# Spectral block of a four-image convolution: two of the four output rows of a Winograd tile computed on GpSimd instead of VectorE

## What is computed

```python
f = fft2(x)                                   # over the two image axes
amp, phase = abs(f), angle(f)
mod_amp = amp * sigmoid(amp @ w_h + b_h) + amp * sigmoid(amp @ w_l + b_l)
spatial = real(ifft2(mod_amp * exp(1j * phase)))
conv = conv3x3(spatial, w_f) + b_f            # SAME padding, 128 -> 128 channels
y = swish(conv) + x
y = (y - mean(y)) * rsqrt(var(y) + 1e-3) * gamma + beta   # over the channels
```

## Time and profile before

| | |
|---|---|
| median of 3 runs | 4309.92 us (4308.83 to 4311.2) |
| the profiled execution: its own time | 4313.71 us |
| its span in the trace | 4311.8 us |
| TensorE busy over the span | 3997.2 us (93%) |
| VectorE busy | 3525.8 us (82%) |
| ScalarE busy | 3160.2 us (73%) |
| GpSimd busy | 2583.8 us (60%) |
| convolution stage of the first image | about 236 to 450 us from the start |
| the fourth image's, the last | about 1509 to 1725 us |

### The profile page before, as it was taken

One profiled execution on the slowest core, in us unless ns is written; L12 is line 12 of the kernel. 1 busy time (PEld: TensorE's weight loads), 2 busy tenths in 40 slices (PEclk: granted clock), 3 DMA queues, 4 the chain that ended last, 5 costly groups with the idle time before them and its releaser, 6 DMA issues.

```text
span 4311.8 us, 95150 instructions
## 1 busy us (share of the span) xinstructions
PE 3997.2 (93%) x31687; PEld 2864.0 (66%) x31687; DVE 3525.8 (82%) x8840; ACT 3160.2 (73%) x4900; POOL 2583.8 (60%) x2713
## 2 busy tenths in 40 slices
PE   7898889789979996599999999999999999999998
PEld 4687568757875786366666666666666666666665
DVE  4568456745775577599999999999999999999997
ACT  4345524552455255599999999999999999999997
POOL 0036103610360047488888888888888888888886
PEclk9999999999999998799999999999999999999999
DMA  2013101400140022111111111111111111111110
GB/s 90 1 51 124 62 1 54 151 32 2 62 165 10 2 65 88 41 40 41 39 41 39 41 39 41 39 41 39 41 39 41 39 41 39 41 39 41 39 41 25
DMA packets 214867, 205.94 MB, mean 48 GB/s; under 512 B 14369, under 2 KB 149153, under 8 KB 214689
## 3 DMA queue, kind: packets, MB, share of 16 engines
q1 hardware_dynamic: 214688, 203.60, 14.4%
HBM read 136.45 MB, written 67.11 MB: 47 GB/s over the span
## 4 chain that ended last, share of the span: by engine, by line
PE 58%; DVE 0%; ACT 0%; POOL 0%; issue 0%; POOLq 0%; DVEq 0%; ACTq 0%
PE g_ps L1039 7%; PE g_ps L1024 6%; PE g_ps L982 6%; PE g_ps L968 5%; PE g_ps L1027 5%; PE g_ps L1056 5%; PE g_ps L999 3%; PE g_ps L1069 3%; PE g_ps L1075 3%; PE g_ps L1048 3%; PE g_ps L1008 3%; PE g_ps L973 3%; PE g_ps L988 2%; PE g_ps L1064 2%; PE g_ps L961 2%; PE g_ps L993 1%
## 5 line engine op out<-in xcount | busy, mean ns | idle before, releaser
L1351 DVE TENSOR_TENSOR g_mmat<-g_emat,g_ps 128x1024 f32<-128x1024 f32 x512 | 599.6, 1212 | 3.7 <-PE g_ps L999 2.7
L1190 ACT ACTIVATE g_emat<-g_ps 128x1024 f32<-128x1024 f32 x512 | 521.3, 1025 | 90.1 <-PE g_ps L1027 88.6
L1294 DVE SCALAR_TENSOR_TENSOR g_acc<-g_ps,g_conv_w,g_acc 128x504 f32<-128x504 f32 (+1 forms) x768 | 555.2, 723 | 11.4 <-ACT g_acc L1153 9.5
L869 POOL TENSOR_TENSOR g_acc<-g_acc,g_tap 128x508 f32<-128x508 f32 x384 | 482.0, 1270 | 128.1 <-DVE g_acc L1294 128.1
L609 POOL MEMSET f_s_hi<- 128x192 f32 x4 | 1.0, 258 | 851.9 <-PE f_ps L344 851.9
L1039 PEld LDWEIGHTS g_ps<-g_mmat,g_dtx 128*32 128x32 f32 x8192 | 192.8, 109 | 310.5 <-issue 164.3
L1024 PE MATMUL g_ps<-g_rz,g_l 128*128 128x512 f32 x1024 | 389.4, 461 | 1.6 <-DVE g_z L1379 1.6
L229 PE MATMUL f_ps<-f_s_hi,f_wf_hi 128*128 128x256 f32 x1152 | 360.7, 313 | 5.0 <-DVE f_s_lo L456 5.0
L1039 PE MATMUL g_ps<-g_mmat,g_dtx 128*32 128x128 f32 x8192 | 329.3, 279 | 0.0
L230 PE MATMUL f_ps<-f_s_lo,f_wf_hi 128*128 128x256 f32 x1152 | 326.5, 283 | 0.0
L231 PE MATMUL f_ps<-f_s_hi,f_wf_lo 128*128 128x256 f32 x1152 | 326.1, 283 | 0.0
(11 more groups left out here) (194 smaller groups left out, 12380.7 us busy)
## 6 DMA issues: line engine op xcount, KB each, us to landing
f_xt<-in_x_cols SPq DMA_DIRECT2D x32, 1024.0 KB, 10.6
f_xres<-in_x SPq DMA_DIRECT2D x128, 256.0 KB, 2.7
z<-f_zout SPq DMA_DIRECT2D x128, 256.0 KB, 2.0
g_zin<-z SPq DMA_DIRECT2D x128, 256.0 KB, 2.6
g_zres<-z SPq DMA_DIRECT2D x128, 256.0 KB, 2.8
out<-g_outb SPq DMA_DIRECT2D x128, 256.0 KB, 2.9
f_wf_raw<-in_w_f SPq DMA_DIRECT2D x1, 576.0 KB, 6.8
g_wx<-in_in_proj_t SPq DMA_DIRECT2D x1, 192.0 KB, 2.4
```

The lines of the kernel that those rows point to most:

```text
L869: pool.tensor_tensor(acc[:, j, :, 1:], acc[:, j, :, 1:], tap1[:, j, :, 0:P - 1], ALU.add).then_inc(add_p[j], 1)
L1190: act.activation(emat[:, g, :].rearrange("p (b n) -> p b n", b=2), ps[:, D_BANK[g]:D_BANK[g] + 2, :], ACT.Exp).then_inc(e_a[g], 1)
L1294: dve.scalar_tensor_tensor(out=acc[:, j, :, k:], in0=four(ps[:, bank, :])[:, :, 0:P - k], scalar=conv_w[:, j, 3 - k:4 - k], in1=acc[:, j, ...
L1351: dve.tensor_tensor(mmat[:, g, :].rearrange("p (h n) -> p h n", h=HEADS), emat[:, g, :].rearrange("p (h n) -> p h n", h=HEADS), ps[:, CB, ...
```

## The change

In `tile_rows` the two instructions L470 and L473 (rows 2 and 1) go. GpSimd gets a new function `inner_rows(k)` of four instructions, which makes the same two rows: two `tensor_scalar` (0.25 * sums near, 0.5 * diffs near, 256 elements each, into `scaled`, a slot of `work` that this stage did not use), a wait for both, and two `tensor_tensor` additions into `conv_y` with the same interleaved writes. It stands last in GpSimd's round k, behind `affine(k-3, ...)` and `root(k-2)`; GpSimd's loop now starts at k = 0. It waits for `sum_done` and `diff_done` of VectorE and for the transposes of batch k-2. Two waits are new elsewhere: `silu(k)` on ScalarE also waits for `inner_done` of batch k, and `tile_rows(k)` on VectorE, before it writes `sums` again, for `inner_done` of batch k-1.

```diff
+        scaled = work[:, 3, :].rearrange("p (a n) -> p a n", a=2)
...
                 def silu(k):
                     act.wait_ge(y_done[k % 2], b * 8 + (k // 2 + 2))
+                    act.wait_ge(inner_done, b * BATCHES + (k + 1))
...
                 dve.wait_ge(mids_ready, done)
+                if k:
+                    dve.wait_ge(inner_done, b * BATCHES + k)
                 dve.tensor_tensor(sums[:, :], first, mids[:, :], ALU.add).then_inc(sum_done, 1)
                 dve.tensor_tensor(diffs[:, :], first, mids[:, :], ALU.subtract).then_inc(diff_done, 1)
                 dve.wait_ge(sum_done, done)
-                dve.scalar_tensor_tensor(out=y[:, :, 2], in0=sums[:, near], scalar=0.25, in1=sums[:, far],
-                                         op0=ALU.mult, op1=ALU.add)
                 dve.wait_ge(diff_done, done)
-                dve.scalar_tensor_tensor(out=y[:, :, 1], in0=diffs[:, near], scalar=0.5, in1=diffs[:, far],
-                                         op0=ALU.mult, op1=ALU.add)
                 dve.wait_ge(conv_mm, done)
...
+                def inner_rows(k):
+                    done = b * BATCHES + (k + 1)
+                    y = conv_y[:, k % 2]
+                    if k >= 2:
+                        pool.wait_ge(vT_mm, b * PARTS + (2 * k - 2))
+                    pool.wait_ge(sum_done, done)
+                    pool.wait_ge(diff_done, done)
+                    pool.sem_inc(waited)
+                    pool.tensor_scalar(scaled[:, 0, :], sums[:, 0:256], 0.25, 1.0, ALU.mult, ALU.mult).then_inc(scaled_done, 1)
+                    pool.tensor_scalar(scaled[:, 1, :], diffs[:, 0:256], 0.5, 1.0, ALU.mult, ALU.mult).then_inc(scaled_done, 1)
+                    pool.wait_ge(scaled_done, b * 2 * BATCHES + (2 * k + 2))
+                    pool.tensor_tensor(y[:, :, 2], scaled[:, 0, :], sums[:, 256:512], ALU.add)
+                    pool.tensor_tensor(y[:, :, 1], scaled[:, 1, :], diffs[:, 256:512], ALU.add).then_inc(inner_done, 1)
...
-                for k in range(2, BATCHES + 3):
+                for k in range(BATCHES + 3):
...
                     if k >= 3:
                         for h in range(2):
                             affine(k - 3, h)
-                    if k < BATCHES + 2:
+                    if 2 <= k < BATCHES + 2:
                         root(k - 2)
+                    if k < BATCHES:
+                        inner_rows(k)
```

More of the change, by code:

```diff
@@ L127, in spectral_block @@
             sem("f_" + n) for n in ("s_mm", "hi_ready", "lo_ready", "pad_ready", "end_ready"))
-        pairs_mm, conv_mm, mids_ready, sum_done, diff_done, ends_done, silu_done, vT_mm, ysum_done, stats_done, mv_ready = (
-            sem("f_" + n) for n in ("pairs_mm", "conv_mm", "mids_ready", "sum_done", "diff_done", "ends_done", "silu_done", "vT_mm",
+        pairs_mm, conv_mm, mids_ready, inner_done, scaled_done, sum_done, diff_done, ends_done, silu_done, vT_mm, ysum_done, stats_done, mv_ready = (
+            sem("f_" + n) for n in ("pairs_mm", "conv_mm", "mids_ready", "inner_done", "scaled_done", "sum_done", "diff_done", "ends_done", "silu_done", "vT_mm",
                                     "ysum_done", "stats_done", "mv_ready"))
```

## The result

The changed kernel takes 4400.3 us (median of 4 runs, 4393.8 to 4401.0) where the kernel before, run beside it, takes 4309.8 us (4308.8 to 4311.2). The ratio is 1.0207, with a 95% interval of 1.0194 to 1.022: slower by about 2.1%. The forecast was 4408 us, in a range of 4374 to 4460. The profiled execution of the changed kernel took 4400.47 us, with a span of 4398.3 us, 86.5 more than before.

What follows compares the result with a forecast made beforehand. The present round was bound on TensorE by hi_part, lo_part, columns; the change closes a GpSimd-ScalarE loop of 13.41 us against 11.48. At 24.6 us an image, 98 us for four, 4309.9 becomes 4408 us, range 4374 to 4460.

Steps and rivals of the forecast that it cites:

- The mechanism: GpSimd and ScalarE: silu waits for inner_rows behind root, GpSimd's next affine waits for center; rounds of 13.41 us, not 11.48.
- the loop: GpSimd's affine, root, inner_rows, then ScalarE's silu, hi_part, center, back to affine, through in-order queues: 13.41 us a round.
- The other new wait: VectorE's tile_rows(k) waiting for inner_rows(k-1): costs nothing, since that was over before silu(k-1).
- Room by shares: Rival: new work fits GpSimd's 3.33 us idle time, 10.8 us within 11.48, and VectorE's relief counts: 4282 us, chance 5%.
- relief term: VectorE without L470 and L473: lo_part starts 0.44 us earlier, cutting TensorE's pause in each of 64 rounds, 28 us.
- the memset's growth: Price of GpSimd's 256-element tensor_scalar: 0.84 ns an element from a memset gave 0.46 us; 0.50 was taken.
- TensorE's clock: Rival: longer TensorE pauses lower its clock; rounds 7 us over 13.4 in a quarter of 52, about 4500 us, chance 3%.
- The first rounds: Rounds 0 to 2 of an image, without affine: the loop is not closed, 0.1 us gained.
- The sum: Whole kernel: 24.7 us more over 13 rounds, less 0.1, is 24.6 an image, 98 us for four: 4408 us.
- The two rules: VectorE-GpSimd SBUF exclusion: affine and root fall from 8.15 to 7.57 us, else 30 us more; and a stride step on GpSimd.
- the rival at 4436 us: GpSimd's additions: each strided element costs half as much again, 0.27 us an addition, 28 us in all; chance 15%.

Runs made afterwards that it cites:

- the first experiment: Changed kernel with VectorE making all four rows again, GpSimd's four new instructions writing unused copies and silu not waiting for them: 4308.0 us, ratio 0.9996.
- The one-row kernels: Changed kernel with GpSimd making one row: row 2 behind root 4352.7 us, row 2 ahead of root 4306.4 us, row 1 ahead of root 4286.4 us.

## Why the prediction was right, and where it was off

**The mechanism** held at each place named: `silu` released by GpSimd, a pause of 3.23 us before `affine` (about 3.2 forecast), L615 at 0.25 us in all rounds, no gap between `affine` and the end of `inner_rows`, TensorE standing before a `columns` for over 2 us. That the loop alone is the cause is shown from both sides: without the wait nothing is lost, with two more additions 1.37 us a round more are lost, and with `root` out of the loop 77 us come back. The other new wait, of `tile_rows`, was forecast to cost nothing, and the first experiment, which keeps it, loses nothing.

**Room by shares**, the rival at 4282 us, is wrong for this change. Its relief term is right for the round, though: leaving the rows out gives rounds of 11.05 us, and 4284 us. (VectorE's own relief was 0.89 us and not 1.01, since the instructions behind did not close up wholly; it made no difference, because `lo_part` then waits for ScalarE.) An engine can have room and its idle time still not be free.

**The terms of the loop**, 13.41 forecast and 13.22 measured:

- `inner_rows` 2.34 us (315.18, the end of L621, to 317.52), not 2.6. The `tensor_scalar` takes 0.40 to 0.41 and starts 0.38 from its neighbour, where I took 0.50 near the memset's growth; the estimate of 0.46 worked out beside it was closer. The wait between the pairs shows as 0.08 us (316.01 to 316.09), not 0.15. The additions are 0.74 and 0.73, as forecast, with starts 0.70 apart.
- `affine` and `root` 7.65 us (307.53 to 315.18), not 7.57; the difference is in `affine`, 5.22 against 5.14, and `root` takes 2.43 in both. `silu` 1.06, `hi_part` 0.37, `center` 1.64 and the hand-overs of 0.09 and 0.07 are as forecast.
- Over 11 full rounds of image 0 the loop gives 0.19 x 11 = 2.1 us less than forecast, and over the last two 0.45 less (25.61, not 26.06).

**TensorE's clock** was put down as a rival at about 4500 us. It did fall, but cost little. The stretches of the changed kernel: the 13 rounds of image 0, then a round at full clock and a stretch of 13.3 us, most of it one round, with a lower one (columns as in the earlier trace rows):

```profile
281.10:452.74 171.64, 137.06 (x963) 130.54 (x961) 115.52 (x370) 83.08 (x180) 124.54 (x159) 0.93 0.32 104
320.75:333.97 13.22, 10.96 (x80) 10.11 (x79) 9.54 (x30) 6.99 (x17) 9.56 (x12) 1.00 0.26 81
...
373.60:386.90 13.30, 11.80 (x79) 11.29 (x79) 9.52 (x30) 6.70 (x16) 9.57 (x12) 0.89 0.24 79
```

The kernel before had 0.99 over its 13 rounds; now it is 0.93. A mean of 0.89 is the lower level, 1.2 GHz, in about a fifth of a round. TensorE has 2.3 to 2.7 us of pauses in a round at full clock to take that up. Where the clock is low just behind the long pause (0.50 from 346 to 349, after three microseconds in which TensorE was busy for 0.58), it does reach the loop (TensorE's and GpSimd's timelines):

```profile
346.25 1.65 PE L218 MATMUL f_ps<-f_idft_h,f_inv 128*128 128x192 f32 x4 [2.67 <-DVE f_s_lo L458]
```

```profile
350.04 1.28 POOL L641 TENSOR_TENSOR f_zout<-f_zout,f_gamma 128x512 f32<-128x512 f32 x1 [0.19 <-ACT f_zout L427]
```

`columns` takes 1.65 us instead of 0.92, the `hi_part` behind it is late, and with it the second `center` and `affine`, by 0.19 us (0.36 in the round at 373.90). That makes two rounds of 13.45 and 13.60, 0.6 us in image 0. The fault of the rival was its size. Of the first 11 rounds 7 show a mean clock below 1.00, none below 0.87, so the low clock fills at most about a quarter of a round; the rival took it for whole rounds, a quarter of them.

**The first rounds.** I forecast 0.1 us gained; the first `affine` came 0.55 us later (281.10 against 280.55). That lies ahead of everything that was changed: VectorE's `lo_part` ahead of the first tile already stands at 250.66 against 249.52, 1.14 us later. Rounds 0 to 2 then won back 0.6 of it, more than I had given them.

**The sum** was 98 us by 24.6 an image. The rounds gave 91.2, the rest minus 4.7, the span 86.5, and the medians 90.5. The error of 8 us is the four small instructions' price (0.26 us x 52 = 13.5 us too dear), with `affine` (0.08 us x 52 = 4.2) and the clock in the other direction, and the stretches between images as scatter. So the forecast came nearer than its worst term, and that part is luck.

**The two rules.** L615 and L616 fell to their quick values in all rounds when L470 and L473 left VectorE, and with these rows back beside `root`, in the first experiment, L618 takes 0.51 us again. The Trainium skill has a rule for this (SBUF — State Buffer, Who interferes with whom): a VectorE instruction with two SBUF inputs and a GpSimd instruction that reads SBUF contend, and the one that comes second waits for the whole of the first. The one-row kernels agree even in that detail: L475 ends 0.50 and 0.51 us behind GpSimd's L642, whether it started 0.42 or 0.86 us before that was over. The sum rested on this: 30 us. The step that the Trainium skill states for widely strided reads (GPSIMD Engine Reference, Performance pitfalls for Q7 kernels) does not show on writes: 0.74 us with writes 16 bytes apart, 0.73 on the addition of the earlier trace rows with dense writes. The page speaks of reads, and the rival at 4436 us, which carried it over to writes, was wrong.

## What to carry to other kernels

Before work moves to an engine with idle time, ask what ends that idle time and who will wait for the moved work. If the one leads to the other through in-order queues, the work is added to every round at its full length, whatever the shares say; measure the loop against the present round. Follow a reordering through every queue that a consumer feeds, the DMA issuer's too, since a store that waits holds back the loads behind it. And of several equal pieces, move the one whose removal leaves no dependent neighbours on the engine it came from.

## What the runs showed of the hardware that I had not expected

- GpSimd's `tensor_scalar` on 256 fp32 elements takes 0.40 to 0.41 us, 0.24 to 0.25 on 8: 0.6 to 0.7 ns an element. Its addition of two operands takes 0.74 us on 256, and writes 16 bytes apart add no more than 0.01 us to it.
- On VectorE an instruction that waits for the semaphore of its neighbour, here the 512-element `diffs`, starts 0.77 to 0.79 us behind it, and 0.60 if it waits for something older. It need not read the result: the changed kernel's L476 reads `sums`, but stands behind the wait for `diffs`, and starts at 0.77. Taking out the instructions that lay beside this wait exposes about 0.17 us of it: the relief was 0.89 us, not 1.01.
- A VectorE instruction with two SBUF inputs that met an addition of GpSimd ended about 0.5 us behind the end of that addition, however early it had started: it took 0.93 and 1.36 us instead of 0.64.
- TensorE's granted clock was below 1.00 in 7 of the first 11 rounds of the changed kernel, where it stood up to 2.7 us at a time at a busy share of 0.8 over the stage; in the same 11 rounds before, with pauses of 0.5 us, it was 1.00 in all.
- Two more places between a load and the stores ahead of it in SyncE's queue were worth 2.15 us a round (13.48 to 11.33) where the stores were late, and nothing where they were not (1.0001, and 4400.4 against 4400.3 us).
